# Two attentions and their MLPs: chunk 1 begun inside the last MLP group, first MLP tiles run between the attention's last operations

## The reference, cut

```python
# A: 16 heads of 16, window 128 within chunks of 128 (own chunk and the one before)
h = layer_norm(x, ln1_g, ln1_b); q, k, v = split(h @ w_qkv.T)
o = softmax(mask(q @ k.T * scale)) @ v
y = x + o @ w_o.T
y = y + gelu(layer_norm(y, ln2_g, ln2_b) @ mlp_w1.T + mlp_b1) @ mlp_w2.T + mlp_b2
x = _layernorm(x + y)
# B, twice: 8 heads of 64; shift_token moves half of the features by one token
q, k, v = split(shift_token(x) @ wqkv)
q, k = rotary_xpos(l2norm(q) * qs, l2norm(k) * ksc)
x1 = x + softmax(mask(8 * q @ k.T)) @ v @ wo
a, g = split(layer_norm(shift_token(x1), lg, lb) @ w1 + b1)
x = x1 + (a * gelu(g)) @ w2 + b2
# at the end
x = _layernorm(x_before_B + x)
```

## Time and profile before

| | us |
|---|---|
| median of 3 runs | 1927.98 |
| the profiled execution | 1934.86 |
| its span, first to last instruction | 1933.1 |
| TensorE busy in it | 1838.1 |
| VectorE busy | 1585.1 |
| ScalarE busy | 1190.8 |
| GpSimd busy | 1087.6 |

### The profile page before, as it was taken

The page is one execution under the profiler, slowest core; times in us unless marked ns, Lnnn a source line. Parts: engine busy times, 40 slices in busy tenths (PEclk is TensorE's granted clock), DMA queues, the critical chain, the costliest instruction groups (busy, mean ns, idle before and its releaser), DMA issues. The chain is left out here.

```text
span 1933.1 us, 43270 instructions
## 1 busy us (share of the span) xinstructions
PE 1838.1 (95%) x15168; PEld 1540.2 (80%) x15168; DVE 1585.1 (82%) x3853; ACT 1190.8 (62%) x3084; POOL 1087.6 (56%) x1040
## 2 busy tenths in 40 slices
PE   6999999989999899999998899989999999979997
PEld 4777777768999788888887788878888888768886
DVE  6888888856987899999997566789999999956776
ACT  5787777754444577777776333347777777733332
POOL 3555444533443677777775255467777867724443
PEclk9999999988999999999999899999999999989999
DMA  2111111003231211111112324241111111122220
GB/s 99 34 31 35 53 34 34 24 18 104 77 106 60 87 48 50 39 50 50 39 45 64 116 81 125 92 132 34 45 50 43 46 50 43 30 80 66 76 76 33
DMA packets 139667, 116.01 MB, mean 60 GB/s; under 512 B 10440, under 2 KB 138704, under 8 KB 138704
## 3 DMA queue, kind: packets, MB, share of 16 engines
q1 hardware_dynamic: 139472, 113.53, 19.1%
HBM read 75.74 MB, written 37.75 MB: 59 GB/s over the span
## 5 line engine op out<-in xcount | busy, mean ns | idle before, releaser
L1627 ACT ACTIVATE b_probs<-masked,neg_max 128x256 f32<-128x256 f32 (+1 forms) x512 | 249.8, 498 | 3.8 <-DVE neg_max L1184 3.8
L520 PE MATMUL psum<-wa_hi,b_h_hi 128*128 128x512 f32 (+1 forms) x576 | 235.4, 409 | 1.3 <-ACT b_h_hi L1547 1.1
L1184 DVE CUSTOM_DVE_ANT_0 masked<-psum,mask 128x256 f32<-128x256 f32 (+1 forms) x512 | 182.3, 412 | 40.8 <-PE psum L774 33.7
L522 PE MATMUL psum<-wa_hi,b_h_lo 128*128 128x512 f32 (+1 forms) x576 | 215.6, 374 | 0.0
L521 PE MATMUL psum<-wa_lo,b_h_hi 128*128 128x512 f32 (+1 forms) x576 | 215.4, 374 | 0.0
L520 PE MATMUL psum<-g_h_hi,wm_hi 128*128 128x512 f32 (+1 forms) x480 | 193.6, 403 | 10.7 <-POOL g_h_lo L1882 7.1
L521 PE MATMUL psum<-g_h_lo,wm_hi 128*128 128x512 f32 (+1 forms) x480 | 192.0, 400 | 0.0
L522 PE MATMUL psum<-g_h_hi,wm_lo 128*128 128x512 f32 (+1 forms) x480 | 191.7, 399 | 0.0
L1833 POOL TENSOR_TENSOR g_in<-g_in,minus_half 128x16 f32<-128x16 f32 x64 | 187.5, 2930 | 0.4 <-DVE g_in L1144 0.4
L1715 ACT ACTIVATE gate<-psum,vec_b 128x512 f32<-128x512 f32 x96 | 66.0, 687 | 177.8 <-PE psum L522 177.7
L520 PE MATMUL psum<-wm_hi,u_hi 128*128 128x256 f32 x576 | 165.6, 287 | 0.0
(11 more groups left out here) (161 smaller groups left out, 5800.1 us busy)
## 6 DMA issues: line engine op xcount, KB each, us to landing
x_mid<-y_out SPq DMA_DIRECT2D x96, 128.0 KB, 1.7
rope_in<-in_rope SPq DMA_DIRECT2D x64, 128.0 KB, 2.2
x_res<-x_state SPq DMA_DIRECT2D x64, 128.0 KB, 2.2
g_in<-x_mid SPq DMA_DIRECT2D x32, 256.0 KB, 3.8
g_old<-x_state SPq DMA_DIRECT2D x16, 512.0 KB, 4.2
out_x<-g_fin SPq DMA_DIRECT2D x15, 512.0 KB, 3.0
w_raw<-in_w_mlp_b SPq DMA_DIRECT2D x2, 2154.0 KB, 8.1
x_in<-in_x SPq DMA_DIRECT2D x32, 128.0 KB, 2.1
```

Of the source, the lines that this page charges most:

```text
L520: nc.tensor.matmul(out, a_hi, b_hi, start=first, stop=False)
L522: return nc.tensor.matmul(out, a_lo, b_hi, start=False, stop=last)
L1184: ins = nc.vector.tensor_tensor_reduce(out[:, at], src[:, at], (mask if now else mask0)[:, at], -1.0, BIG, ALU.add, ALU.min, neg_max[:, r, ...
L1627: ins = nc.scalar.activation(out, src, ACT.Exp, bias=neg_max[:, r, k:k + 1], scale=-1.0, accum_out=row_sum[:, n % 2, 4 * r + k:4 * r + k + 1])
```

## The change

It moves work across all five seams, on all queues.

- **Into the end of attention A**: the statistics of the first MLP group go to step 30 round 2, the power to step 30 round 3, normalization to step 31 round 0, the transposes of z to step 31 round 1, gain and bias to round 2, the splits to round 3 and step 32. Hidden tiles 0 to 3 of the first group are issued at the ends of the four rounds of step 32 (`EARLY` is 4).
- **Into the end of both attentions B**: statistics and power to step 31 round 0, normalization and z transposes to round 1, gain, bias and splits to step 32 round 0, hidden tiles 0 and 1 to the end of step 32 round 1, ahead of the last output projection. The spread of the inverse sums of chunk 31 now comes ahead of its last values.
- **Into the last MLP group**: q and k of chunk 1 are projected between the halves of `down`; its copies, norms, rotations and powers follow. `scale_rotated(0)` goes ahead of the second half of the product sum. `rotate_q(1)` goes between `add_old` and `finish_stats`. `finish` goes from step -1 to step 0, behind `scale_rotated(1)`. The transposes of x of chunk 2 now wait for all of `y_added`.
- **SP**: the last store, its wait and the zero row go into step 0 of the next attention.
- The PSUM banks of the MLPs are renamed for this (`TURNS`, `Z`, `FIRST_Z`), and every projection waits by the new order (`b_projected`).

```diff
@@ class Mlp
-MLP_A = Mlp(4 * D, False)
-MLP_B = Mlp(int(D * 4 * 2 / 3), True)
+MLP_A = Mlp(4 * D, False, (0, 4, 5, 6, 7, 3), (1, 2), (0, 1), 4)
+MLP_B = Mlp(int(D * 4 * 2 / 3), True, (0, 2, 6, 7, 1, 3), (4, 5), (0, 2), 2)
...
@@ sp_attention
-            sp.wait_ge(zero_rows_stored, layer * 32 + 16)
             load_mlp_weights(sp, io["w_mlp_b"][layer * P:layer * P + P, :], layer + 2)
...
                 if b_chunk(s + 5):
                     sp.wait_ge(S["rope_ready"], g0 + s + 2)
                     load(s + 5)
+                if s == 0:
+                    sp_mlp(sp, *mlp_behind(layer), None if layer == 0 else layer - 1, opening="last")
+                if s == 4:
+                    sp.wait_ge(zero_rows_stored, layer * 32 + 16)
...
@@ pe_attention_a
                 if 0 <= i - 1 < 4 * NCH:
                     transpose_probs(i - 1)
-                if (s, r) == (NCH, 2):
+                if (s, r) == (NCH - 1, 1):
+                    pe.wait_ge(S["kt_copied"], 2 * NCH)
+                    pe.wait_ge(S["qt_copied"], 2 * NCH)
+                    pe.wait_ge(S["o_lo"], NCH - 2)
+                    pe_mlp(pe, MLP_A, MA, None, opening="z")
+                if s == NCH and r > 0:
                     pe.wait_ge(S["exp_ready"], 4 * NCH)
-                    pe_mlp(pe, MLP_A, MA, None, opening=True)
+                if s == NCH:
+                    pe_mlp(pe, MLP_A, MA, None, opening=r)
@@ pe_attention
+                if n == 2:
+                    pe.wait_ge(behind["y_added"], 4 * NGRP * max(layer, 1))
...
+            if opening == 3:
+                project_q(1)
+                project_k(1)
+                return
...
+                if (s, r) == (NCH, 1):
+                    spread_inverse(s - 1)
                 if b_chunk(s - 1):
                     values(s - 1, r)
...
-                    if b_chunk(s + 2) and s + 2 > 0:
+                    if b_chunk(s + 2) and s + 2 > 1:
                         project_q(s + 2)
                         project_k(s + 2)
...
-                    if b_chunk(s - 1):
+                    if b_chunk(s - 1) and s < NCH:
                         spread_inverse(s - 1)
...
+                if (s, r) == (NCH - 1, 1):
+                    pe.wait_ge(S["kt_copied"], g0 + NCH)
+                    pe.wait_ge(S["qt_copied"], g0 + NCH)
+                    pe_mlp(pe, MLP_B, MB, layer, opening="z")
                 if (s, r) == (NCH, 1):
-                    pe_mlp(pe, MLP_B, MB, layer, opening=True)
+                    pe_mlp(pe, MLP_B, MB, layer, opening=0)
+                    pe.wait_ge(S["pt_act"], 2 * (g0 + NCH))
+                    pe.wait_ge(S["pt_dve"], 2 * (g0 + NCH))
+                    pe_mlp(pe, MLP_B, MB, layer, opening=1)
@@ pe_mlp
                 down(t, 0)
+                if overlap:
+                    pe_attention(pe, next_layer(layer), opening=3)
                 down(t, 1)
...
-            if opening:
-                transpose_z(base)
+            if opening == "z":
+                transpose_z(base, c.FIRST_Z)
                 return
-            pe.wait_ge(wm_split, SPLIT if layer is None else layer * SPLIT + 2 * SPLIT)
-            group(base, True, False)
+            if opening is not None:
+                if opening == 0:
+                    pe.wait_ge(wm_split, SPLIT if layer is None else layer * SPLIT + 2 * SPLIT)
+                    pe.wait_ge(S["h_hi"], base + 1)
+                    pe.wait_ge(S["h_lo"], base + 1)
+                    pe.wait_ge(S["h_lo_pool"], base + 1)
+                hidden(base, opening, False)
+                return
+            group(base, True, False, c.EARLY)
@@ dve_attention_a
+                if (s, r) == (NCH - 2, 2):
+                    dve_mlp(v, MLP_A, MA, None, opening=0)
+                if (s, r) == (NCH - 1, 0):
+                    dve_mlp(v, MLP_A, MA, None, opening=1)
+                if (s, r) == (NCH - 1, 2):
+                    dve_mlp(v, MLP_A, MA, None, opening=2)
                 if (s, r) == (NCH, 0):
-                    dve_mlp(v, MLP_A, MA, None, opening=0)
...
+                    dve_mlp(v, MLP_A, MA, None, opening=3)
@@ dve_attention
+            if opening == 3:
+                norms(1, 1)
+                scale_rotated(0)
+                norms(1, 0)
+                return
+            if opening == 4:
+                rotate_q(1)
+                return
...
                 if r == 0:
-                    if s == -1:
-                        scale_rotated(0)
-                        h_low(2)
-                        dve_mlp(v, *((MLP_A, MA, None) if layer == 0 else (MLP_B, MB, layer - 1)), opening="finish")
-                    elif b_chunk(s + 1):
+                    if b_chunk(s + 1) and s + 1 > 1:
                         rotate_q(s + 1)
-                        if b_chunk(s + 3):
-                            h_low(s + 3)
+                    if b_chunk(s + 3) and s + 3 > 1:
+                        h_low(s + 3)
+                    if b_chunk(s + 1) and s + 1 > 0:
                         scale_rotated(s + 1)
+                    if s == 0:
+                        dve_mlp(v, *mlp_behind(layer), None if layer == 0 else layer - 1, opening="finish")
                     if b_chunk(s - 1):
                         invert_sums(s - 1)
                         copy_probs(s - 1, 1)
+                    if s == NCH - 1:
+                        dve_mlp(v, MLP_B, MB, layer, opening=0)
+                    if s == NCH:
+                        dve_mlp(v, MLP_B, MB, layer, opening=2)
+                        dve_mlp(v, MLP_B, MB, layer, opening=3)
...
                         scale_o(s - 1)
+                    if s == NCH - 1:
+                        dve_mlp(v, MLP_B, MB, layer, opening=1)
...
@@ dve_mlp
                 add_product(t, slot, 0)
+                if overlap:
+                    dve_attention(v, next_layer(layer), opening=3)
...
             if next_layer(layer) < LAYERS:
+                dve_attention(v, next_layer(layer), opening=4)
                 finish_stats(base + (NGRP - 1), 1)
@@ act_attention
                 copy_qk(0, 1)
+                copy_qk(1, 0)
+                copy_qk(1, 1)
                 return
...
+                    if s == NCH:
+                        act_mlp(a, MLP_B, MB, layer, opening=True)
...
@@ pool_attention_a
-                if (s, r) == (NCH, 0):
+                if (s, r) == (NCH - 2, 3):
                     pool_mlp(pool, MLP_A, MA, None, opening=0)
-                if (s, r) == (NCH + 1, 0):
+                if (s, r) == (NCH - 1, 3):
                     pool_mlp(pool, MLP_A, MA, None, opening=1)
...
@@ pool_attention
-                tables(0)
-                rotate_k(0)
-                inverse_norms(0)
+                for n in range(2):
+                    tables(n)
+                    rotate_k(n)
+                    inverse_norms(n)
                 return
...
+                    if s == NCH - 1:
+                        pool_mlp(pool, MLP_B, MB, layer, opening=0)
+                    if s == NCH:
+                        pool_mlp(pool, MLP_B, MB, layer, opening=1)
```

153 lines of the change are left out of this document (77 added, 76 removed).

## The result

| | before | after |
|---|---|---|
| median, us (17 runs each) | 1930.97 | 1924.92 |
| lowest to highest | 1925.88 to 1934.67 | 1923.03 to 1927.47 |
| the profiled execution's span | 1933.1 | 1923.1 |

The ratio is 0.9968, with a 95% interval of 0.996 to 0.9975: 6.1 us faster. The 1927.98 us of the forecast was the median of the first 3 of these 17 runs of the kernel before. The forecast was 15.6 us (1912.4, a ratio of 0.9919). The sign was right, the size was not. The time is close to rival 2's 1925.5, but rival 2 had a gain of 2.5 us.

A forecast was written before the change was run, and what follows sets the result against it. TensorE, busy 1838.1 of 1933.1 us, was taken as the bound. Seams: -9.7 - 1.7 - 7.3 + 1.4 - 7.1 = -24.4 us at full clock; with 8.8 us of low clock remaining, -15.6, giving 1912.4 us, range 1904 to 1925.5.

The forecast's parts named there:

- rival 2: All seams: the idle only moves and the clock falls as before; -2.5 us, 1925.5 us, chance 0.20.
- Seam A: From attention A to its MLP: early hidden tiles fill the waits, 19.0 us instead of 28.7, -9.7 at full clock.
- the stretch at 413.9: A low-clock stretch standing before Seam A, which the forecast left as it is.
- the 6.6 us of clock cost: Low-clock cost inside Seam A, half of 13.14 us busy time; forecast to go, with no stretch remaining there.
- M0 and M1: Seams from the later attentions to their MLPs: 29.7 instead of 37.0 us and 29.5 instead of 36.6, -7.3 and -7.1.
- The two idles: At M0 and M1: TensorE idle 2.8 us before the z transposes and 2.9 before the spread of inverse sums.
- B0 and B1: Seams from last hidden block to scores of chunk 1: -1.7 and +1.4 us at full clock, VectorE's queue delaying project v.
- one stretch in each seam, at 2.2 us: Low clock remaining in B0 and B1 and M0 and M1: one stretch each costing 2.2 us, 8.8 in all.
- Rival 1: All seams: the clock stays full everywhere; -24.4 us, 1904 us, chance 0.14.
- Rival 3: All seams: VectorE's queue holds TensorE and the low clock returns; slower, +8.6 us, 1936.5 us, chance 0.14.

The follow-up runs named there:

- e2: The kernel before with only the early first MLP tiles between the last operations of attention A, nothing at the other seams; 1923.4 us, ratio 0.9956.
- e1: The changed kernel with the part undone that begins chunk 1 of the later attentions inside the last MLP group; 1915.9 us, ratio 0.9916.
- e7: The changed kernel with o_low(28) put ahead of inverse_norms(31) on GpSimd at step 30 of both later attentions; 1923.4 us, ratio 0.9948.
- e12: The changed kernel with low parts, statistics and first maxima ahead of rotate_q(1), finish later, and at B1 the second add_product ahead of scale_rotated(0); 1912.2 us, 0.9894.
- e3: The kernel before with only chunk 1 of both later attentions begun inside the last MLP group; 1941.6 us, ratio 1.0046.
- e11: The changed kernel with o_low(28) ahead of inverse_norms(31) on GpSimd and scale_rotated(31) behind invert_sums(29) and copy_probs(29,1) on VectorE; 1917.2 us, ratio 0.992.
- e4: The changed kernel with rotate_q(1) and finish_stats behind h_low(2), k_t_low(0) and q_t_low(0) on VectorE at B0 and B1; 1912.2 us, ratio 0.9905.
- e6: The changed kernel with gain_bias (VectorE) and h_high (ScalarE) ahead of copy_probs(31,1) at M0 and M1; 1917.6 us, ratio 0.9916.

## Why the prediction was wrong

**Idle and clock.** By the pages, TensorE idled 95.0 us before (1933.1 - 1838.1) and 92.2 after (1923.1 - 1830.9): 2.8 us less, where the forecast had 2.5. Its busy time, which holds the clock's cost, fell by 7.2 us, where the forecast had 13.1. So the idle sum was right and the clock was not.

**Seam A, -9.7: near, measured -8.5 (e2).** The idles left from the first hidden tile on are 0.88, 0.98 and 0.52 us, 2.4 in all against 2.5 predicted, and the tail starts later by about the 2.1 us forecast: the transposes of probabilities at 422.44 stood at 419.95 in the second profile of the kernel before, at full clock in both. The shortening between the two first profiles was 12.8, since the stretch at 413.9 that I had left as it is went too. Wrong in kind was the 6.6 us of clock cost: the second profile of the kernel before shows that part of it was that one execution's, which was 3.9 us above the median, and the median could not lose it. There, 6.6 us less of halved busy time (25.15 / 2 less 11.96 / 2) was worth only 4.35 us. Wrong too was "none in A, where no idle above 1 us is left": 10 of 13 profiles have a stretch of 3.4 us there.

**M0 and M1, -7.3 and -7.1 at full clock: right.** Without a low stretch M0 is -8.1 (e1, e7, e12), with one of 6.8 us -5.4, where I had -5.1. The two idles are 1.92 and 3.05 us against 2.8 and 2.9: normalization took 1.37 us there and not 2.32. By whole runs the two seams gave 7.7 us (e1 less e2) where 10.0 was forecast. In e2 they are already 1.4 and 1.3 us shorter without an edit there, by fewer low stretches; no run shows why.

**B0 and B1: the failing step.** Mechanism, list and place were right, and so was the idle time: 38.20 - 32.64 = 5.6 us in B0 and 39.70 - 29.66 = 10.0 in B1, 15.6 together where I had 6.5 + 8.8 = 15.3. The term that was mis-sized is the clock: one stretch in each seam, at 2.2 us. Halving the busy time of the stretches gives (8.17 + 3.40) / 2 = 5.8 us at B0 and (5.22 + 3.40) / 2 = 4.3 at B1, 10.1 instead of 4.4; in the second profile 3.3 and 5.9, 9.2 together. I had taken the mean of the stretches that cost 1.7 and 2.7, which stood at single idles of 2.3 to 3.2 us, and left out the two of 13.6 and 10.3 us, which stood at pairs of idles (3.65 and 2.3, 3.65 and 2.5). Yet at B1 I had myself predicted a pair, 2.2 and 4.9. The list on VectorE also ran longer, 10.6 us from scaling to low part instead of 9.3, with the old sum at 1.73 instead of 1.23; TensorE's first wait was longer as well (3.52 instead of 2.2). A second fault was where I let the seam end, at the scores of chunk 1. One stretch and a wait of 1.58 us (`values` of chunk 0) lie behind it in B0, 2.5 us in all. Predicted +4.1 for both, measured +8.9 (e3).

**Step 30: not in the forecast.** Its idle of 2.7 us was there before, without a low stretch; now the clock falls behind it in some executions, 1.5 us each, in e2 too, where of the computing engines' work nothing but seam A is changed. Why it falls there now and did not before stays open. e11, which shortens the idle, has no fall there. I had looked only at places that the change touches.

**The sum.** By whole runs: A 1.2 us short of the forecast, M0 and M1 2.3, the chunk-1 part 4.8, and the parts together 1.2 off their sum: 9.5 us. With some 3 us of error on each part, only the chunk-1 part is clearly off.

**The rivals.** Rival 2 (1925.5, +21.9 for a clock that falls as before) has nearly the right time, in part by luck: its gain of 2.5 us is 3.6 short of the 6.1 measured, and its base of 1927.98 was 3 us below the median of 17 runs. Its mechanism is half right: the clock's bill was 19.3 us after and 21.9 before, but it went from A to B0, B1 and step 30 instead of staying put. Rival 1 is refuted by the earlier trace rows's answer above. Rival 3's mechanism is real at B0 and B1 and is what e4 removes, but it decides the sign of the chunk-1 part only, not that of the whole change. The chance of 0.20 for rival 2 was too low: my own list had idles of 2.8 us and more at four seams, and I had written that idles of 2.25 to 3.65 us stood at nearly every fall.

## What to carry to other kernels

When work is moved ahead in a queue, look for the small operation behind it on which the busiest engine waits: here 0.42 us of VectorE behind 5 us of work wanted only later held TensorE for 4.7 us, and the order alone, at two seams, was worth 12 us. Price an idle of TensorE at its length and the low clock behind it (in e6 2.4 us of idle came with 2.7 of clock), and ask whether an idle that stays elsewhere will be the next behind which the clock falls. Time a change of many parts part by part: -8.5, -7.7 and +8.9 us hide behind one -6.1.
